# Chunk 0's graph attention moved into the last but one attention iteration, chunk 1's into the recurrence's first half

## The chip, the cores and the metric

One core of one Trainium2 chip runs the kernel. The metric is the device time of one execution in microseconds; the kernel before takes 1593.96 us (median of 3 runs, 1591.88 to 1594.06).

## The reference, cut to what matters

Input x is 128 graphs of 64 tokens with 256 features; adj is one 64x64 adjacency for all. Four residual blocks follow one another, each on `h = relu(layernorm(x))`:

```python
x = x + L0(h)   # attention, 8 heads, q/k/v/o products, scores masked by adj
x = x + L1(h)   # attention, 8 heads; o + layernorm(o) * gamma + beta
x = x + L2(h)   # graph attention: hw = h @ W
                # e = leaky_relu(s1[i] + s2[j], 0.2) * adj; att = softmax(e)
                # elu(att @ hw + beta * hw)
x = x + L3(h)   # gated recurrence, 3 steps:
                # av = [adj h, adj h];  z = sigmoid(av w3 + h u3)
                # r = sigmoid(av w4 + h u3);  hv = tanh(av w5 + (r*h) u5)
                # h = (1-z)*h + z*hv
```

## The kernel before, in words

x stays in on-chip memory as 64 tiles of 128 tokens; four tiles (8 graphs) are a chunk, so there are 16 chunks (`CHUNKS`). The engines run separate programs, one block each (`@block.tensor` and so on), and meet at semaphores. The order on each engine is written by hand; nothing is scheduled by a planner.

**Attention.** One software-pipelined loop (`iterations`, `body(i, ...)`) runs over T = 32 chunk-steps: 16 of L0, then 16 of L1. In iteration i the tensor engine (PE) makes the scores of i, transposes the softmax output p of i-1 (`p_transposes`), transposes the normalised rows of i+1, projects the output of i-2 (`o_products`), multiplies p by v for i-1 (`values`) and projects q, k, v of i+1. The vector engine (DVE) masks and takes maxima (`mask_and_max`), sums, makes the low parts of split operands (`o_low`), takes outputs (`take_first`, `take_out`), makes statistics (`o_stats`) and adds the normalised output (`final_sum`). The scalar engine (ACT) copies out of PSUM, takes exponentials and normalises. POOL subtracts maxima (`shift`), divides (`normalise`), turns statistics into rstd (`norms`, `norm`), scales by gamma (`scale`) and issues two accumulating DMAs (`beta_to_x`, `o_to_x`). Each fp32 product is three matmuls of high and low parts (`product`, line 99).

**PSUM** has two tensors of four banks: `scores`, also called `high`, and `ring`. A p transpose of the drained pipeline (i = T) writes ring banks 0 and 1 only when the oT held there has been read by `o_low`.

**Graph attention** of chunk c: `graph_rows` transposes normalised rows, `graph_high`/`graph_low` split them into g_hT, four `graph_product` make hw, `graph_s2` makes s2, `graph_scores` e and its maximum, `g_shift` and `g_exponential` the exponential, `graph_attention` att, `graph_attT` transposes it, `copy_attT` adds beta times identity, `graph_aggregate` makes y, and `graph_out` on ACT and DVE applies elu and adds to x. Chunks 2 to 15 are done inside the recurrence, but chunks 0 and 1 stand in the tail behind the attention loop.

**Recurrence.** Two chunks are in flight; a *half* is half a step's work for one of them (`half(s)`, `halves`). `enter` brings a chunk in from its normalised rows (r_hn). Half 0 starts chunk 0 with `hu = u3 hp`, the neighbour sums with adjT (`agg`), then w4 (r), w3 (z) and w5; the next half starts with hu of chunk 1 and then `u5` on r*h (rhp) of chunk 0. In the tail, the graph attention of chunks 0 and 1 and the last attention iterations T-1, T, T+1 are interleaved by a hand-written list per engine; on PE it begins:

```python
iterations(pe, body)
scores_piece(T - 1)
p_transposes(T - 1, 1)
o_products(T - 1, 1)
pe.wait_ge(s_masked, (T - 1) * R + 2)
graph_rows(0, high)
values(T - 1, 1)
```

## Time and profile before

| | us |
|---|---|
| median of 3 runs | 1593.96 |
| lowest, highest | 1591.88, 1594.06 |
| the profiled execution | 1595.16 |
| its span, first to last instruction | 1593.1 |
| PE busy | 1510.5 (95%) |
| DVE busy | 1243.9 (78%) |
| ACT busy | 993.0 (62%) |
| POOL busy | 533.7 (34%) |

The span is 2.06 us shorter than the profiled execution's own time, which is 1.2 us above the median. Attention fills the span up to about 600 us and the recurrence from about 640 us. Busy shares are of the span; a wait is idle time of an engine, put down to the instruction that released it. The granted clock of PE is given as a share of 2.4 GHz. All times below are from the start of the span.

### The profile page before, as it was taken

What the parts mean: (1) busy time and instruction counts of PE and PEld (TensorE: products, weight loads), DVE (VectorE), ACT (ScalarE), POOL (GpSimd) and SP (SyncE); (2) the same over time, 40 slices, a digit from 0 to 9 for tenths busy, and PEclk for the clock granted to TensorE, in tenths of its full rate; (3) what the DMA queues carried; (4) which work ended last, traced back from release to release, by engine and by line L of the source; (5) the groups of instructions that cost most, each with busy time, mean ns of one, the idle gap of its engine ahead of it and who ended that gap; (6) DMA issues with size and microseconds to landing.
All of it is one profiled execution on the core that took longest, in us unless ns stands there. A gap on an engine that the chain in (4) does not pass through costs nothing.

```text
span 1593.1 us, 40455 instructions
## 1 busy us (share of the span) xinstructions
PE 1510.5 (95%) x16248; PEld 1299.4 (82%) x16248; DVE 1243.9 (78%) x2511; ACT 993.0 (62%) x1793; POOL 533.7 (34%) x622
## 2 busy tenths in 40 slices
PE   3899999899999987799999999999999999999997
PEld 3789989798888876588888888888888888888885
DVE  2787887988899986677877877877777777778666
ACT  3676677667777774565666566655665566566553
POOL 1666766667787893300101111111111111111000
PEclk9999999999999998899999999999999999999998
DMA  9200000003322242100000000000000000000000
GB/s 251 82 3 0 0 0 1 15 16 61 61 53 53 56 78 29 27 0 1 27 1 1 27 0 0 26 0 0 26 0 0 26 0 0 27 1 0 27 1 26
DMA packets 36760, 40.12 MB, mean 25 GB/s; under 512 B 11840, under 2 KB 31808, under 8 KB 36672
## 3 DMA queue, kind: packets, MB, share of 16 engines
q0 software_dynamic: 4608, 16.78, 5.6%
q1 hardware_dynamic: 32064, 22.10, 4.8%
q8 instruction: 64, 1.05, 0.3%
q14 instruction: 24, 0.20, 0.0%
HBM read 13.71 MB, written 8.39 MB: 14 GB/s over the span
## 4 chain that ended last, share of the span: by engine, by line
PE 68%; DVE 15%; ACT 7%; issue 5%; POOL 4%; DMA 1%; SPq 0%; DVEq 0%; POOLq 0%; ACTq 0%
PE ring L99 30%; PE scores L99 23%; PE scores L1545 3%; PE ring L1343 2%; PE scores L1307 2%; DVE rhp_lo L1196 2%; PE ring L1490 2%; DVE total L955 2%; POOL s L530 1%; PE ring L1380 1%; ACT rhp_hi L824 1%; ACT later_w L814 1%; PE ring L1508 1%; PE ring L1463 1%; ACT later_w L808 1%
## 5 line engine op out<-in xcount | busy, mean ns | idle before, releaser
L1196 DVE TENSOR_TENSOR rhp_lo<-r,rhp_hi 128x1024 fp32r<-128x1024 f32 x48 | 58.8, 1225 | 157.0 <-ACT rhp_hi L824 157.0
L530 POOL TENSOR_TENSOR s<-s,mx 128x512 f32<-128x512 f32 x128 | 137.9, 1102 | 46.3 <-DVE mx L951 46.3
L536 POOL TENSOR_TENSOR s<-s,rtotal 128x512 f32<-128x512 f32 x128 | 131.4, 1056 | 36.7 <-DVE rtotal L957 36.5
L594 POOL TENSOR_TENSOR r_var_eps<-r_mean_var,eps 128x4 f32<-128x4 f32 x16 | 8.1, 509 | 384.3 <-DVE r_mean_var L1105 384.3
L669 ACT ACTIVATE s<-s 128x512 f32<-128x512 f32 x128 | 78.4, 644 | 76.1 <-POOL s L530 75.9
L839 ACT ACTIVATE hv<-scores,bias 128x512 f32<-128x512 f32 x96 | 66.1, 689 | 83.6 <-PE scores L99 83.6
L946 DVE SCALAR_TENSOR_TENSOR s<-scores,mask 128x512 f32<-128x512 f32 x128 | 87.2, 681 | 32.4 <-PE scores L1307 32.4
L808 ACT ACTIVATE later_w<-ring 128x512 f32<-128x512 f32 x64 | 34.8, 595 | 121.9 <-PE ring L1508 121.9
L681 ACT ACTIVATE pT<-ring 128x512 f32<-128x512 f32 x128 | 66.1, 604 | 47.1 <-PE ring L1343 47.1
L951 DVE TENSOR_REDUCE mx<-s 128x8 f32<-128x512 f32 x128 | 87.9, 686 | 4.4
L857 ACT ACTIVATE r<-r,bias_half 128x512 f32<-128x512 f32 x96 | 64.3, 717 | 37.7 <-DVE r L1221 37.7
L99 PE MATMUL scores<-rhp_hi,u5T_hi 128*128 128x512 f32 x192 | 80.4, 419 | 4.0 <-DVE rhp_lo L1196 1.8
L955 DVE TENSOR_REDUCE total<-s 128x8 f32<-128x512 f32 x128 | 82.6, 645 | 0.0
L1232 DVE TENSOR_TENSOR later_w<-scores,hu 128x512 f32<-128x512 f32 x96 | 64.4, 686 | 19.6 <-PE scores L99 18.8
L99 PE MATMUL ring<-agg_hi,w4T_hi 128*128 128x512 f32 x192 | 78.9, 411 | 0.0
L99 PE MATMUL scores<-agg_hi,w3T_hi 128*128 128x512 f32 x192 | 78.3, 408 | 0.0
L594 POOL TENSOR_TENSOR g_var_eps<-g_mean_var,eps 128x4 f32<-128x4 f32 x16 | 7.3, 457 | 209.5 <-DVE g_mean_var L1105 209.5
L99 PE MATMUL scores<-agg_hi,w5T_hi 128*128 128x512 f32 x192 | 77.0, 401 | 0.0
L99 PE MATMUL ring<-agg_lo,w4T_hi 128*128 128x512 f32 x192 | 76.2, 397 | 0.0
L99 PE MATMUL ring<-agg_hi,w4T_lo 128*128 128x512 f32 x192 | 76.2, 397 | 0.0
L99 PE MATMUL scores<-agg_hi,w5T_lo 128*128 128x512 f32 x192 | 75.9, 395 | 0.0
L99 PE MATMUL scores<-rhp_lo,u5T_hi 128*128 128x512 f32 x192 | 75.8, 395 | 0.0
(295 smaller groups left out, 5251.2 us busy)
## 6 DMA issues: line engine op xcount, KB each, us to landing
x<-beta_less_one POOLq DMA_DIRECT2D x16, 512.0 KB, 4.6
x<-o POOLq DMA_DIRECT2D x16, 512.0 KB, 6.5
out_x<-x SPq DMA_DIRECT2D x16, 512.0 KB, 2.9
x<-in_x SPq DMA_DIRECT2D x1, 6656.0 KB, 30.5
later_w<-in_L_gnn_w_w SPq DMA_DIRECT2D x3, 512.0 KB, 7.2
x<-in_x SPq DMA_DIRECT2D x1, 1024.0 KB, 10.9
stage<-in_L_gnn_w_qkv SPq DMA_DIRECT2D x3, 256.0 KB, 3.0
x<-in_x SPq DMA_DIRECT2D x1, 512.0 KB, 3.5
```

The source lines that it names most:

```text
L99: last = pe.matmul(out, s, m, start=(begins and n == 0), stop=(ends and n == len(terms) - 1))
L530: pool.tensor_tensor(sr, sr, mx[:, r, :].unsqueeze(2).to_broadcast([P, CT * 2, N]), ALU.subtract).then_inc(s_shifted, 1)
L536: pool.tensor_tensor(sr, sr, rtotal[:, r, :].unsqueeze(2).to_broadcast([P, CT * 2, N]), ALU.mult).then_inc(p_ready, 1)
L669: act.activation(s[:, par, r, :, :, :], s[:, par, r, :, :, :], ACT.Exp).then_inc(p_exp, 1)
L681: act.activation(pT[:, r, :, :].rearrange("p t q -> p (t q)"), ring[:, r, :], ACT.Copy).then_inc(pT_copied, 1)
L839: act.activation(hv[:, m, :], high[:, 2 + m, :], ACT.Tanh, bias=bias[:, 2, m:m + 1])\
L857: act.activation(r[:, m, :], r[:, m, :], ACT.Tanh, bias=bias_half[:, 1, m:m + 1], scale=0.5)\
L946: dve.scalar_tensor_tensor(sr(par, r), scores[:, r, :].rearrange("p (a k) -> p a k", k=N), SCALE, masks[layer_of(i, lay)][:].unsqueeze(1). ...
L951: dve.reduce_max(mx[:, r, :], sr(par, r), AX.X).then_inc(s_max, 1)
L955: dve.reduce_sum(total[:, r, :], sr(par, r), AX.X).then_inc(p_total, 1)
L1196: dve.tensor_tensor(rhp.lo[:], r[:], f32(rhp.hi[:]), ALU.subtract).then_inc(rh_lo_ready, 1)
L1232: dve.tensor_tensor(z[:, m, :], high[:, m, :], hu[:, m, :], ALU.add).then_inc(z_added, 1)
```

## The change

Chunk 0's graph attention starts in `body(T - 2)`: rows normalised first on ACT, transposed on PE behind the values, split into new buffers (`g_hT_first`, in the part of later_w that is free by then), multiplied between the k and v products. The rest of chunk 0 stands in iteration T-1; chunk 1's products in iteration T. Chunk 1's attT transpose, aggregate, output and entry are moved into the recurrence's first half. On ACT the last two `o_normalise` move into that half; on DVE the last three `final_sum` stand behind the first half (one) and the second (two). `hw_next` and `h_a` get other places in memory; `enter`, `graph_high`, `graph_low` and others take the PSUM bank as an argument.

```diff
@@ placement
+        g_hT_first = Parts(plan, "g_hT_first", [P, FT, CW], start["later_w"] + 4096)
-        hw_next = sb("hw_next", [P, CT, WX], F32, start["s"] + 8192)
+        hw_next = sb("hw_next", [P, CT, WX], F32, start["w_ext"])
-        h = [sb(f"h_{q}", [P, FT, CW], F32, start["o_n"] + 4096 * n) for n, q in enumerate("ab")]
+        h = [sb("h_a", [P, FT, CW], F32, start["w1o_hi"]), sb("h_b", [P, FT, CW], F32, start["o_n"])]
@@ ACT, body
+                    if isinstance(i, int) and i == T - 2:
+                        graph_normalise(0, 0)
                     o_normalise(i, par, lay)
...
+                        if i == T - 2:
+                            graph_high(0, high, 0, g_hT_first)
...
+                        if isinstance(i, int) and i == T - 2:
+                            for t in range(CT):
+                                copy_hw(0, t, high, 2)
                         copy_v(i + 1, 1 - par)
@@ ACT, half
+                    if s.first:
+                        o_normalise(T + 1, 1, 1)
...
+                    if s.first:
+                        graph_out(1, high, 2)
+                        norm_rows(rn, r_hn[1], 1, 1)
+                        enter(1, 1)
                     if s.graph_norm is not None:
                         graph_normalise(s.graph_norm, 0 if s.k == 0 else 1)
+                    if s.first:
+                        o_normalise(T + 2, 0, 1)
@@ DVE, body
+                    if isinstance(i, int) and i == T - 2:
+                        graph_low(0, high, 0, g_hT_first)
                     o_stats(i, par, lay)
                     final_sum(i, par, lay)
+                    if isinstance(i, int) and i == T - 2:
+                        rows_stats(gn, 1, x_final)
@@ DVE, half
+                    if s.first:
+                        copy_attT(1, high, 2)
...
+                    if s.first:
+                        graph_out(1, high, 2)
+                        recurrence_stats(1)
...
+                    if s.first:
+                        enter(1, 1)
@@ DVE, behind the halves
                     half(s)
                     if s.first:
+                        final_sum(T + 1, 1, 1)
+                    if isinstance(s.n, int) and s.n == 1:
                         final_sum(T + 2, 0, 1)
                         final_sum(T + 3, 1, 1)
                         dve.wait_ge(x_final, CHUNKS)
@@ PE, body
+                    if i == T - 2:
+                        pe.wait_ge(s_masked, (i + 1) * R)
+                        graph_rows(0, high)
...
+                        if isinstance(i, int) and i == T - 2:
+                            pe.wait_ge(g_hT_lo_ready, FT)
+                            pe.wait_ge(gw_lo_ready, 2)
+                            for t in range(CT):
+                                wait(pe, hw_copied, t - 1)
+                                graph_product(0, t, high, 2, g_hT_first)
@@ PE, half
+                    if s.first:
+                        graph_attT(1, high, 2)
...
+                    if s.first:
+                        graph_aggregate(1, high, 2, hw_next)
...
+                        if s.first:
+                            pe.wait_ge(x_plus_pos, 4)
                         for m in range(FT):
                             product(pe, high[:, 2 + m, :], columns(wT["w5"], m), moving(agg), ends=False)
+                    if s.first:
+                        pe.wait_ge(hu_copied, FT)
+                        enter(1, 1)
@@ PE, tail
                 scores_piece(T - 1)
                 p_transposes(T - 1, 1)
+                pe.wait_ge(s_masked, (T - 1) * R + 1)
+                graph_s2(0, high, 0, g_hT_first)
                 o_products(T - 1, 1)
...
                 values(T - 1, 1)
...
+                graph_attT(0, high, 0)
                 pe.wait_ge(s_masked, T * R)
...
+                graph_rows(1, high, 2)
+                graph_aggregate(0, high, 0)
                 p_transposes(T, 0)
...
                 pe.wait_ge(g_hT_lo_ready, 2 * FT)
                 for t in range(CT):
                     if t >= 2:
                         pe.wait_ge(hw_copied, CT + t - 1)
...
+                    graph_product(1, t, high, 2)
+                o_products(T, 1)
+                graph_s2(1, high, 2)
+                values(T, 0)
                 o_products(T + 1, 1)
...
                 pe.wait_ge(x_plus_pos, 2)
...
+                enter(0, 0, high, 0)
                 halves(pe, half)
@@ POOL, tail
+                norms(T - 1, 1, 1)
+                norm(gn, 1, 1)
                 pool.wait_ge(v_ready, T * 2)
+                pool.memset(att[:], 0.0).then_inc(att_cleared, 1)
                 pool.memset(adjT[:], 0.0).then_inc(adj_cleared, 1)
...
+                shift(T - 1, 1, 0)
+                shift(T - 1, 1, 1)
+                g_shift(0)
+                beta_to_x(T - 1, 1)
+                o_to_x(T - 1, 1, 1)
+                shift(T - 1, 1, 2)
+                shift(T - 1, 1, 3)
+                scale(T - 1, 1, 1)
+                for q in range(R):
+                    normalise(T - 1, 1, q)
+                norm(rn, 0, 0)
```

The order on DVE in iteration T-1, before, from its last mask to the second split of graph rows (L951 maximum, L973 o_low, L1114 graph_low):

```order
L951 TENSOR_REDUCE mx<-s 128x8
L966 TENSOR_TENSOR o<-ring,out_bias_93 128x512
L973 TENSOR_TENSOR oT_lo<-ring,oT_hi 128x4x2x64 x2
L955 TENSOR_REDUCE total<-s 128x8
L957 RECIPROCAL rtotal<-total 128x8
L955 TENSOR_REDUCE total<-s 128x8
L957 RECIPROCAL rtotal<-total 128x8
L1114 TENSOR_TENSOR g_hT_lo<-scores,g_hT_hi 128x512 x2
```

o_low stands right behind the last output and ahead of the sums. After the change, the same place from the last mask on (L972 maximum, L1175 copy_attT, L976/L978 a sum, L1183/L1188 graph_out, L1125 statistics, L994 o_low):

```order
L972 TENSOR_REDUCE mx<-s 128x8
L1175 TENSOR_TENSOR attT<-scores,beta_ident 128x512
L987 TENSOR_TENSOR o<-ring,out_bias_93 128x512
...
L1183 SCALAR_TENSOR_TENSOR x<-scores,x 128x512 x2
L1188 TENSOR_TENSOR x<-x,later_w 128x1024
...
L1125 BN_STATS r_stats<-x 128x6 x4
L1128 MEMSET carrier 128x1
L1130 BN_AGGR r_mean_var<-r_stats 128x2 x4
L987 TENSOR_TENSOR o<-ring,out_bias_93 128x512
L994 TENSOR_TENSOR oT_lo<-ring,oT_hi 128x4x2x64 x2
```

Two sums stand in each of the first two gaps. o_low now comes behind the four sums, chunk 0's graph output and its statistics.

The order on ACT around the first half, before (L692 o_normalise, L768 normalised rows, L818/L829 the hu copies, L835 agg_hi):

```order
L801 ACTIVATE h_a<-scores 128x512
L692 ACTIVATE o_n<-o,shift_by,rstd 128x256 x4
L768 ACTIVATE r_hn_b<-x,r_shift_by,r_rstd 128x256 x4
L692 ACTIVATE o_n<-o,shift_by,rstd 128x256 x4
L818 ACTIVATE hu<-ring 128x512
L829 ACTIVATE hu<-ring 128x512
L835 ACTIVATE agg_hi<-scores 128x512 x2
```

and after the change (L706 o_normalise, L789 normalised rows, L839/L850 the hu copies, L856 agg_hi, L813/L816 chunk 1's graph_out):

```order
L822 ACTIVATE h_a<-scores 128x512
L706 ACTIVATE o_n<-o,shift_by,rstd 128x256 x4
L839 ACTIVATE hu<-ring 128x512
L850 ACTIVATE hu<-ring 128x512
L856 ACTIVATE agg_hi<-scores 128x512 x2
L706 ACTIVATE o_n<-o,shift_by,rstd 128x256 x4
L880 ACTIVATE r<-r,bias_half 128x512 x2
L813 ACTIVATE later_w<-scores 128x512 x2
L816 ACTIVATE later_w<-later_w 128x1024
L789 ACTIVATE r_hn_b<-x,r_shift_by,r_rstd 128x256 x4
```

One block of four stands ahead of the hu copies instead of three; chunk 1's rows are normalised behind r.

## Rows read from the trace of the kernel before

**Rows 1.** Stretches: us, busy PE PEld DVE ACT POOL, PEclk, DMA share, GB/s.

```profile
583.60:672.00 88.40, 62.01 (x706) 54.66 (x706) 59.67 (x141) 49.18 (x95) 39.34 (x54) 0.85 0.25 37
...
672.00:1560.00 888.00, 882.71 (x4642) 739.89 (x4642) 687.73 (x1215) 535.47 (x929) 87.52 (x122) 1.00 0.03 9
```

**Rows 2.** PE's waits in 583 to 672 us: total, times, longest.

```profile
PE ring L1463 <- ACT hu L829: 9.2, 1, 9.2
...
PE scores L1482 <- DVE att L1143: 6.6, 2, 4.8
...
PE scores L99 <- DVE g_hT_lo L1114: 5.9, 1, 5.9
```

**Rows 3.** Stretches again, same columns, for the granted clock (PEclk).

```profile
599.03:604.80 5.77, 5.77 (x26) 5.67 (x27) 4.45 (x15) 1.37 (x4) 4.95 (x8) 0.50 0.18 1
...
614.84:624.30 9.46, 9.46 (x66) 8.85 (x66) 6.12 (x11) 4.11 (x8) 0.61 (x1) 1.00 0.00 0
...
629.20:642.10 12.90, 8.89 (x26) 6.85 (x27) 8.36 (x20) 5.48 (x10) 0.79 (x3) 0.63 0.00 1
...
654.83:659.50 4.67, 4.67 (x15) 3.78 (x16) 2.97 (x11) 2.97 (x6) 2.39 (x4) 0.50 0.21 39
```

**Rows 4.** The same view: the graph products, and the twelve w3 matmuls.

```profile
615.25:618.25 3.00, 3.00 (x28) 3.00 (x26) 1.46 (x3) 1.16 (x3) 0.00 (x0) 1.00 0.00 0
...
660.88:663.68 2.80, 2.80 (x14) 2.26 (x13) 2.48 (x4) 2.18 (x5) 0.00 (x0) 1.00 0.00 0
```

**Rows 5.** PE's timeline: start us, us, line, operation, count, [idle before].

```profile
583.60 1.59 PE L1307 MATMUL scores<-kT,qT 32*64 32x64 f32 x128
...
585.12 1.97 PE L1343 MATMUL ring<-ident,s 128*128 128x128 f32 x16
...
639.38 0.80 PE L99 MATMUL ring<-hp_a_hi,u3T_hi 128*128 128x512 f32 x1 [3.16 <-DVE hp_a_lo L1168]
...
671.86 0.48 PE L99 MATMUL scores<-rhp_hi,u5T_hi 128*128 128x512 f32 x1
```

**Rows 6.** DVE's timeline, same columns.

```profile
582.76 1.62 DVE L1000 TENSOR_TENSOR x<-x,o_n 128x1024 f32<-128x1024 f32 x1
...
597.73 1.24 DVE L1114 TENSOR_TENSOR g_hT_lo<-scores,g_hT_hi 128x512 fp32r<-128x512 f32 x2
...
606.22 0.86 DVE L1123 TENSOR_TENSOR e<-scores,hw 64x256 f32<-64x256 f32 x2 [2.54 <-PE scores L99]
...
608.03 0.42 DVE L1132 TENSOR_REDUCE g_mx<-e 128x4 f32<-128x256 f32 x1
...
612.93 1.85 DVE L1143 TENSOR_TENSOR att<-e,g_rtotal 64x256 f32<-64x256 f32 x2
...
624.71 1.41 DVE L1100 BATCH_NORM_STATS2 r_stats<-x 128x6 f32<-128x256 f32 x4
...
628.28 0.85 DVE L1143 TENSOR_TENSOR att<-e,g_rtotal 64x256 f32<-64x256 f32 x2
...
664.49 2.35 DVE L1000 TENSOR_TENSOR x<-x,o_n 128x1024 f32<-128x1024 f32 x2
...
691.76 1.22 DVE L1196 TENSOR_TENSOR rhp_lo<-r,rhp_hi 128x1024 fp32r<-128x1024 f32 x1 [3.63 <-ACT rhp_hi L824]
```

**Rows 7.** ACT's timeline, same columns.

```profile
575.42 0.63 ACT L669 ACTIVATE s<-s 128x512 f32<-128x512 f32 x1 [0.98 <-POOL s L530]
...
635.60 1.06 ACT L795 ACTIVATE later_w<-later_w 128x1024 f32<-128x1024 f32 x1
...
643.00 2.08 ACT L692 ACTIVATE o_n<-o,shift_by,rstd 128x256 f32<-128x256 f32 x4 [4.40 <-POOL shift_by L524]
```

**Rows 8.** POOL's timeline, same columns.

```profile
611.72 2.36 POOL L560 TENSOR_TENSOR o_n<-o_n,gamma 128x1024 f32<-128x1024 f32 x1 [2.57 <-ACT o_n L692]
...
647.94 0.19 POOL L594 TENSOR_TENSOR r_var_eps<-r_mean_var,eps 128x4 f32<-128x4 f32 x1
...
649.48 0.20 POOL L600 TENSOR_TENSOR r_shift_by<-r_minus_mean,r_rstd 128x4 f32<-128x4 f32 x1
```

More of the change, by code:

```diff
@@ L567, in body @@
                         norm(gn, 0, 0)
-                    if isinstance(i, int) and i == T - 1:
-                        norm(gn, 1, 1)
                     if exists(i):
@@ L843, in half @@
                         copy_hw(s.graph_a, 1)
-                    if s.enters is not None:
+                    if s.enters is not None and not s.first:
                         enter(s.enters, s.other)
+                    if s.first:
+                        o_normalise(T + 1, 1, 1)
                     if s.norm is not None and s.k == 4:
@@ L1249, in _ @@
                 iterations(dve, body)
-                rows_stats(gn, 1, x_final)
-                for q in range(3):
-                    mask_and_max(T - 1, 1, q, 1)
-                take_first(T - 1, 1, 1)
-                mask_and_max(T - 1, 1, 3, 1)
+                mask_and_max(T - 1, 1, 0, 1)
+                mask_and_max(T - 1, 1, 1, 1)
+                graph_scores(0, high, 0)
+                mask_and_max(T - 1, 1, 2, 1)
+                dve.wait_ge(att_cleared, 1)
+                dve.tensor_scalar(beta_ident[:], ident[:], g_beta[:, 0:1], None, ALU.mult).then_inc(beta_ident_ready, 1)
@@ L1255, in _ @@
+                graph_attention(0)
+                mask_and_max(T - 1, 1, 3, 1)
+                dve.wait_ge(beta_ident_ready, 1)
+                copy_attT(0, high, 0)
+                take_first(T - 1, 1, 1)
+                sums(T - 1, 1, 0)
+                sums(T - 1, 1, 1)
+                graph_out(0, high, 0)
+                sums(T - 1, 1, 2)
+                sums(T - 1, 1, 3)
+                recurrence_stats(0)
                 take_out(T - 3, 1, 1, 1)
                 o_low(T - 2)
-                sums(T - 1, 1, 0)
@@ L1258, in _ @@
-                sums(T - 1, 1, 1)
-                graph_low(0, high)
-                sums(T - 1, 1, 2)
-                sums(T - 1, 1, 3)
+                graph_low(1, high, 2)
                 o_stats(T - 1, 1, 1)
-                final_sum(T - 1, 1, 1)
-                dve.tensor_scalar(beta_ident[:], ident[:], g_beta[:, 0:1], None, ALU.mult).then_inc(beta_ident_ready, 1)
-                graph_scores(0, high, 2)
-                graph_low(1, high)
                 take_first(T, 0, 1)
                 take_out(T - 2, 1, 0, 1)
-                dve.wait_ge(att_cleared, 1)
@@ L1270, in _ @@
-                graph_attention(0)
+                o_stats(T, 0, 1)
+                final_sum(T - 1, 1, 1)
+                graph_scores(1, high, 2, hw_next)
                 o_low(T - 1)
-                dve.wait_ge(beta_ident_ready, 1)
-                copy_attT(0, high, 2)
-                graph_scores(1, high, 0, hw_next)
-                graph_out(0, high, 2)
-                recurrence_stats(0)
+                graph_attention(1)
                 take_first(T + 1, 1, 1)
                 take_out(T - 1, 1, 1, 1)
-                graph_attention(1)
@@ L1280, in _ @@
-                copy_attT(1, high, 0)
+                enter(0, 0, high, 0)
+                o_stats(T + 1, 1, 1)
                 final_sum(T, 0, 1)
-                graph_out(1, high, 0)
-                enter(0, 0, high)
-                o_stats(T, 0, 1)
-                recurrence_stats(1)
-                o_stats(T + 1, 1, 1)
-                final_sum(T + 1, 1, 1)
-                dve.wait_ge(x_final, CHUNKS - 2)
-                halves(dve, first_half)
+                dve.wait_ge(x_final, CHUNKS - 4)
@@ L1291, in _ @@
+                halves(dve, half_and_rest)
             @block.tensor
@@ L1539, in half @@
                         if s.first:
-                            pe.wait_ge(x_plus_pos, 4)
                             pe.wait_ge(adj_loaded, 32)
@@ L1554, in half @@
                         pe.wait_ge(hu_copied, (n + 1) * FT)
-                    if s.enters is not None:
+                    if s.enters is not None and not s.first:
                         enter(s.enters, s.other)
+                    if s.first:
+                        graph_attT(1, high, 2)
                     if s.graph_a is not None:
```

112 lines of the change are left out of this document (45 added, 67 removed).

## The prediction

> **What bounds the kernel now.** Read the busy time by stretch first [rows 1]: from 672 us on the tensor engine (PE) works 882.71 of 888.00 us, so whatever is won or lost before is carried to the end unchanged; in 583.6 to 672 us, where the change sits, it works only 62.01 of 88.40. The list of waits and the timeline say where the other 26 us go [rows 2, 5]: four releasers make up 24.9 us, the longest single wait being 9.2 us for the scalar engine's (ACT) copy of hu. The granted clock adds a second loss [rows 3]: after the waits of 5.9 and 9.2 us matmuls ran at the lower of the two levels (0.50, 1.2 GHz), for 5.77 us after the first and 4.67 us after the last, while after the 1.8 us wait for the first att the clock stayed at 1.00. Between 629.2 and 642.1 us, behind the 4.8 us wait for the second att, it was 0.63 in the mean, with work broken by waits of 0.9 and 3.2 us.
>
> **Unit prices.** The 24 graph products of 128x258 took 3.0 us and twelve matmuls of 128x512 2.80 us (0.233 each) [rows 4]; from the first of these I take 2.85 for the 24 projection matmuls of 128x256 and 1.45 for 16 of half the size. 16 transposes cost up to 1.9 us, the scores 1.5 [rows 5]. At the lower clock each doubles. Vector engine (DVE): one PSUM subtraction or bias add of 128x512 0.6, the graph score block 2.25, statistics of one chunk 1.75, a 128x1024 addition 1.25; a mask and its maximum 1.3, a sum and its reciprocal 0.8, from the same widths [rows 6]. ACT: four rows of 128x256 2.0, a 128x1024 pass 1.0, a 128x512 one half of it [rows 7]. The norm steps on POOL take 1.74, from 647.94 to 649.68 [rows 8].
>
> **The sum, station by station**, on the clock of the profiled execution. T is 32.
>
> 1. *Iteration T-2.* PE gets 8 transposes (0.95) after the values, and 24 graph products (2.9) between k and v. ACT normalises the graph rows (2.0) ahead of o_normalise and the exponentials; the wait for POOL's shift that stood there (0.98 [rows 7]) covers half of it, so o_high and the last exponential are 0.9 later. DVE runs its four sums and then graph_low (1.2 for both halves), which ends at 583.05; PE reaches the products at 581.75 and so waits 1.3. Scores of T-1 start at 583.60+0.95+1.3+2.9 = 588.75, **5.15 later** than now.
> 2. *Iteration T-1.* Scores 1.5, transposes 1.9, graph_s2 1.4: 593.55. On DVE graph scores 2.25, mask 2 1.3, beta_ident 0.25, attention 1.5 (two att instructions of 0.43, a sum, a reciprocal), mask 3 1.3, copy_attT 0.65: 600.85. PE meanwhile runs its projections and values and waits 1.1 for att. Aggregate 1.6: 602.5. The two waits for the graph's own chain (5.9 and 1.8) have become one of 1.1, and the half-clock products of now run at full clock in T-2.
> 3. *The new hole.* The transposes of T need o_low(T-2), which on DVE stands behind first output 0.6, two sums 1.6, graph_out(0), two sums 1.6, recurrence statistics 1.75, an output 0.6. graph_out ends at 606.3 (ACT, which has two exponentials and graph_high(1) before them, ends its relus and Exp at 605.05; then the addition). So the first half of o_low ends at 610.85 and PE idles **8.35**. That is longer than any wait now before the first half, and the lower clock follows as it did after 5.9.
> 4. PE from 610.85: 16 transposes at half clock 3.45, products of chunk 1 eleven slow and thirteen fast 3.95, projection 2.85, s2 1.4, values 1.45: 623.95. DVE then does output, statistics of o 1.85, final_sum 1.25, graph_scores(1) 2.25 and o_low(T-1) 1.2, ending 628.3; PE idles 4.35 and, as after 4.8 now, comes back slow: projection of T+1 5.1, entry transposes 1.5, four ACT copies and DVE's hp_a_lo: 636.85. Now the recurrence's first product starts at 639.38 [rows 5], so up to here only **2.5** is won.
> 5. *First half.* Now ACT keeps PE 9.2 waiting, because o_normalise, norm_rows and o_normalise stand ahead of the hu copies [rows 2, 7]. After the change one o_normalise (2.0) stands there and fits under the products. hu 2.8, neighbour sum 1.85, agg_hi and agg_lo 1.15, w4 2.8, aggregate(1) 1.6, w3 2.8, w5 2.8: PE ends at 652.6, now 666.5. But chunk 1 isn't in yet: from its y at 647.0 relus and Exp 2.25, addition 1.25, statistics 1.75, POOL 1.75, norm_rows 2.05, transposes, ACT copies and hp_b_lo 3.25: 659.3. PE idles 3.5 and 2.2 around the transposes; I take the clock low behind this.
> 6. *Second half.* hu twelve slow 5.1, graph transposes and neighbour sum 2.7: 667.1. On ACT graph rows 2.0, o_normalise 2.0, z 1.3, hu 0.5, rhp_hi 1.0 after 658.65, then DVE's rhp_lo 1.25: 666.7. The u5 product, which starts at 671.86 now [rows 5], starts at **667.0**: 4.9 won.
> 7. *Sharing between DVE and POOL.* The addition x<-x,o_n took 1.2 alone (two in 2.35) and 1.62 beside POOL work; the pair of att took 0.85 alone and 1.85 beside POOL's 2.36 us scaling [rows 6, 8]. In stations 2 to 4 POOL's shifts, scale and normalise stand beside the att and addition. Between nothing and 1.4 us, I take 0.7, since the first att meets DMA issues rather than scaling.
>
> All moved pieces exist in both: 8+8 transposes, 48 products, the Exps, the additions, the POOL DMAs (two in each of T-1 and T, one in T+1 and T+2), the SP queue's adjT loads. The memset that starts the latter comes some 10 us earlier and the product that needs them only at 640. New buffers (hw_next, h_a, g_hT_first) add no instruction. I cost at nothing: final_sum(T+1), 1.2, now behind the first half on DVE, and the last two final_sums (2.35 together, now after the first half, then after the second [rows 6]); what hides them there is DVE's wait of 3.63 before rhp_lo. If that cover is gone, they cost up to 2.35.
>
> Sum: 4.9 - 0.7 = **4.2 us** less. The profiled execution took 1595.16 (span 1593.1, 2.06 around it), the median is 1593.96; against the median that is **1589.8**, 0.26% faster. The bound for "same" is 0.2%, 3.2 us: about what a measurement of this kernel can tell from no change.
>
> **Rivals.**
> *A, the gain is mostly given back in the second half.* DVE enters it late, with one 1.2 us final_sum before and 2.35 behind; the 3.63 us cover is partly used up by ACT being 0.7 us later than now against PE's u5. Then 2.35 more shows: 4.2 - 2.35 = 1.85 won, 1592.1. For it: the wait for rhp_hi is the last thing before u5. Against: after 672 us DVE is busy 77% only [rows 1].
> *B, the 4.35 us wait of station 4 leaves the clock high.* It is shorter than the 4.8 that the clock fell with; the 1.8 us wait left it at 1.00 [rows 2, 3]. Projection and transposes of station 4 then cost 3.6 and not 6.6, minus what ACT has to do anyway: 2.3 more won, 1587.5.
> *C, slower: the clock stays low through the first half.* It did so now over 12.9 us, with work cut up by short waits [rows 3]; the changed first half has waits of 1.95 and 0.65. If the clock doesn't return before w4, hu costs 2.8 more, the neighbour sum 1.8 and w4 2.8, 0.7 of it hidden: 6.7 lost against 4.2 won, 1596.5. It decides at 637 us: the clock must be back by the first hu. Against: 6.6 us of unbroken work stand ahead of that, and in both unbroken stretches of now the clock came back, after 5.77 and 4.67 us [rows 3].
> *D, POOL and DVE block each other whole:* the pair of att then waits for all of a POOL instruction like the 2.36 us scaling, and the two additions lose 0.43 each [rows 6, 8]: 3.2 instead of 0.7, so 1.7 won, 1592.3. Against: the slowest att pair on record lost 1.0. SBUF — State Buffer in the Trainium skill (section Who interferes with whom) has this rule: a DVE instruction with two SBUF inputs and a GpSimd instruction that reads SBUF lock each other out for the whole instruction. The trace agrees that the two meet, with 1.85 against 0.85, and not yet with the full length.
>
> **Numbers.** Forecast 0.47, A 0.18, B 0.15, C 0.10, D 0.10. The range from 1586.0 to 1595.0 takes in the forecast, A, B and D with a microsecond or more of room, and leaves out C. Faster by over 0.2%: forecast 0.43, B 0.14, a part of A and D 0.03: 0.60. Same: 0.32. Slower: 0.08.
>
> **What would show it.** In the changed profile: a wait of PE for g_hT_lo near 582 us of 1 to 2 us; scores of T-1 near 588.8; the longest wait (7 to 10 us) on the transposes of T, released by DVE's oT_lo; the first u3 product near 637; hardly a wait for hu; 3 to 4 us for r_hn_b's transposes behind the first w5; u5 near 667; PE 1.00 busy from there. It is wrong if the hole is over 11 us, if the first u3 product is not before 639.4, or if waits in the loop grow.

## The result, and the profile after

| | before | changed |
|---|---|---|
| median | 1593.95 us (4 runs, 1591.88 to 1594.06) | 1603.88 us (4 runs, 1600.81 to 1607.28) |
| ratio | | 1.0066 [1.0044, 1.0088] |
| profiled execution | 1595.16, span 1593.1 | 1607.28, span 1605.2 |

The change is **slower**, by 0.66%; 1603.88 lies outside the range given. The profiled execution of the changed kernel is the slowest of its four, so its profile shows 12.1 us of difference where the medians show 9.9.

First the stretches of the changed kernel, beside [rows 1]: iteration T-2 from its scores to those of T-1, from there to the first u5 product, and 888 us behind it (us, busy time of PE, PEld, DVE, ACT and POOL, PEclk, DMA share, GB/s).

```profile
572.71:595.47 22.76, 21.22 (x385) 19.26 (x384) 20.00 (x53) 15.88 (x32) 19.72 (x26) 1.00 0.25 48
595.47:683.46 87.99, 60.47 (x673) 52.85 (x673) 53.02 (x125) 44.72 (x84) 35.73 (x48) 0.79 0.25 37
683.46:1571.46 888.00, 882.36 (x4635) 739.47 (x4636) 691.40 (x1218) 535.98 (x930) 87.81 (x122) 1.00 0.03 9
```

The recurrence is as before: PE works 882.36 of 888 us, against 882.71. The stretch from the scores of T-1 to u5 takes 87.99 us where it took 88.26 (583.60 to 671.86 [rows 5]), so the 5.36 us that T-2 has grown by aren't earned back. I call the whole from the scores of T-2 to the first u5 product **the tail**: 105.66 us before (from 566.20 to 671.86), 110.75 after. PE's waits in it (engine, line, released by: total, times, longest):

```profile
PE ring L1375 <- DVE oT_lo L994: 7.6, 1, 7.6
PE ring L99 <- DVE hp_a_lo L1193: 6.2, 1, 6.2
PE ring L99 <- DVE oT_lo L994: 4.6, 1, 4.6
PE ring L1504 <- ACT r_hn_b L789: 3.6, 1, 3.6
PE scores L1523 <- DVE att L1168: 2.3, 1, 2.3
PE ring L99 <- DVE hp_b_lo L1193: 2.0, 1, 2.0
PE scores L99 <- DVE g_hT_first_lo L1139: 1.4, 1, 1.4
PE ring L99 <- DVE agg_lo L1229: 1.0, 1, 1.0
```

Of the waits of before [rows 2], the one for hu is gone, those for att are down to one of 2.3 and the one for g_hT_lo to 1.4. The hole on o_low(T-2) is there as foreseen. The second line is not in the sum at that size. It stands between these two rows of PE's timeline, the first product of T+1 and the first u3:

```profile
637.16 0.55 PE L99 MATMUL ring<-w1o_hi,oT_hi 128*128 128x256 f32 x1 [4.60 <-DVE oT_lo L994]
...
649.41 0.80 PE L99 MATMUL ring<-hp_a_hi,u3T_hi 128*128 128x512 f32 x1 [6.23 <-DVE hp_a_lo L1193]
```

The timelines of DVE and ACT show what it is:

```profile
635.72 1.29 DVE L994 TENSOR_TENSOR oT_lo<-ring,oT_hi 128x512 fp32r<-128x512 f32 x2
...
646.87 1.29 DVE L987 TENSOR_TENSOR o<-ring,out_bias 128x512 f32<-128x512 f32 x2 [8.44 <-ACT o_n L706]
648.08 1.28 DVE L1193 TENSOR_TENSOR hp_a_lo<-scores,hp_a_hi 128x512 fp32r<-128x512 f32 x2
```

```profile
643.75 0.60 ACT L821 ACTIVATE hp_a_hi<-scores 128x512 fp32r<-128x512 f32 x1
644.23 0.62 ACT L822 ACTIVATE h_a<-scores 128x512 f32<-128x512 f32 x1
644.71 2.08 ACT L706 ACTIVATE o_n<-o,shift_by,rstd 128x256 f32<-128x256 f32 x4
```

`take_first(T + 1)` on DVE writes the buffer `o` that `o_normalise(T)` on ACT reads. The change puts that o_normalise behind `enter(0, 0, high, 0)` on ACT, and take_first stays ahead of enter on DVE. (The text on the change ahead of the prediction says that the last two o_normalise move. A third moves too, this one: in the kernel before it stands ahead of `g_exponential(0)` and is done at 611.6, 28 us before the first u3.) So ACT must finish the entry of chunk 0 and then 2.08 us of rows before DVE may begin two subtractions that PE is waiting for. Its input had been ready since POOL's shift at 625.1.

A second part of the difference stands where no code was changed. From the first scores of the program to those of T-2 the profile of before takes 532.07 us and this one 539.20. PE's granted clock there, in two stretches of the changed kernel and then in the same two of the kernel before:

```profile
300.00:320.00 20.00, 17.02 (x324) 15.24 (x327) 16.67 (x41) 10.82 (x21) 13.56 (x17) 0.83 0.09 28
420.00:440.00 20.00, 19.30 (x306) 17.11 (x306) 14.46 (x38) 12.50 (x25) 12.62 (x14) 0.83 0.14 26
```

```profile
300.00:320.00 20.00, 16.77 (x351) 15.12 (x349) 18.37 (x45) 11.66 (x23) 12.70 (x16) 1.00 0.10 29
420.00:440.00 20.00, 20.00 (x366) 17.89 (x365) 18.75 (x47) 16.01 (x32) 15.93 (x17) 1.00 0.28 53
```

So of the 12.1 us between the two profiled executions 5.1 are the tail, 7.1 lie ahead of the change, and the ends cancel. What the second part is had to be asked as well.

### The profile page after: what moved, and what is told of

The parts are those of the page before. It is cut to its first block, busy times and chain, and to the rows that moved or that the text cites. A ratio compares the mean times of both kernels' runs of the same rounds, so it can differ in the third digit from the quotient of the medians.

```text
span 1605.2 us, 40456 instructions
## 1 busy us (share of the span) xinstructions
PE 1519.1 (95%) x16248; PEld 1306.1 (81%) x16248; DVE 1244.1 (78%) x2511; ACT 994.3 (62%) x1793; POOL 534.5 (33%) x622
## 4 chain that ended last, share of the span: by engine, by line
PE 70%; DVE 13%; ACT 8%; issue 4%; POOL 3%; DMA 1%; SPq 0%; DVEq 0%; POOLq 0%; ACTq 0%
PE ring L99 32%; PE scores L99 23%; PE scores L1585 3%; PE ring L1375 3%; PE scores L1336 2%; DVE rhp_lo L1221 2%; PE ring L1412 2%; ACT rhp_hi L845 2%; PE ring L1531 2%; ACT later_w L835 1%; DVE total L976 1%; ACT later_w L829 1%; PE ring L1504 1%; PE ring L1549 1%; POOL s L531 1%
## 5 line engine op out<-in xcount | busy, mean ns | idle before, releaser
L829 ACT ACTIVATE later_w<-ring 128x512 f32<-128x512 f32 x64 | 34.8, 596 | 121.0 <-PE ring L1549 121.0
L972 DVE TENSOR_REDUCE mx<-s 128x8 f32<-128x512 f32 x128 | 87.9, 686 | 4.4
L976 DVE TENSOR_REDUCE total<-s 128x8 f32<-128x512 f32 x128 | 82.5, 645 | 0.0
L99 PE MATMUL scores<-rhp_hi,u5T_lo 128*128 128x512 f32 x192 | 75.8, 395 | 0.0
L99 PE MATMUL scores<-agg_hi,w3T_lo 128*128 128x512 f32 x192 | 75.8, 395 | 0.0
```

The source lines that it names most:

```text
L99: last = pe.matmul(out, s, m, start=(begins and n == 0), stop=(ends and n == len(terms) - 1))
L972: dve.reduce_max(mx[:, r, :], sr(par, r), AX.X).then_inc(s_max, 1)
L976: dve.reduce_sum(total[:, r, :], sr(par, r), AX.X).then_inc(p_total, 1)
```

## Experiments

In all profiles the way from the first u5 to the end takes 921.2 to 922.6 us, so the tail can be read by itself. Beside every run below stand 17 to 29 executions of the kernel before, from which its ratio is taken; their medians were 1593.4 to 1594.6. "Up to scores T-2" counts from the first scores of the program.

| kernel | median us (runs) | ratio [95%] | up to scores T-2 | tail |
|---|---|---|---|---|
| before, again | 1594.08 (10) | 0.9990 [0.9975, 1.0005] | 531.7 | 105.6 |
| change, again | 1602.02 (10) | 1.0050 [1.0028, 1.0071] | 534.1 | 110.0 |
| e1 o_n first | 1594.04 (10) | 0.9990 [0.9973, 1.0007] | 531.8 | 107.1 |
| e6 o_low alone | 1593.97 (10) | 1.0007 [0.9998, 1.0016] | 532.0 | 103.2 |
| e2 both orders | 1587.83 (4) | 0.9957 [0.9941, 0.9974] | 532.8 | 97.7 |
| e3 first half only | 1594.17 (10) | 0.9997 [0.9985, 1.0009] | 537.2 | 101.2 |
| e4 e2 + o_low(T-1) | 1586.56 (12) | 0.9955 [0.9939, 0.9970] | 533.3 | 95.3 |
| e5 e2 + added work | 1583.30 (6) | 0.9937 [0.9923, 0.9952] | 532.3 | 94.2 |
| e9 change + added work | 1594.67 (10) | 1.0006 [0.9993, 1.0019] | 531.9 | 104.2 |
| e8 e4 + e5 | 1581.07 (6) | 0.9918 [0.9902, 0.9934] | 530.9 | 92.9 |
| e7 change, 305 us | 1597.03 (11) | 1.0015 [1.0004, 1.0027] | 530.8 | 110.6 |
| e10 before, 305 us | 1591.17 (12) | 0.9979 [0.9966, 0.9991] | 528.5 | 106.1 |

### Both kernels again

> The kernel before as a kernel of its own, for a second trace. Theory U: the scores of T-2 may come late here too in one run or another (568 us or more). Theory L: 566.2 within 0.5 us. The ratio to the kernel before is 1.000 within 0.002.

> The changed kernel once more, untouched. Theory U (part of the loss lies ahead of the change and comes and goes): the scores of iteration T-2, at 572.7 us in the first profile against 566.2 before, start elsewhere this time, and the time moves with them by as much. Theory L (the loss ahead of the change belongs to this program): again 572 to 573 us and 1601 to 1607. Both: from the scores of T-2 to the first u5 product again about 110.7 us, against 105.7 before.

The tails repeat within 0.8 us: 105.6 and 110.0. The part ahead doesn't: 531.7 and 534.1, after 532.1 and 539.2. The ten runs of the changed kernel spread from 1596.5 to 1609.1, and they go with the granted clock: its mean over an execution is 0.987 to 0.989 in the three fastest (up to 1597.2) and 0.979 in the two slowest (1608.8 and 1609.1). The kernel before has 1590.8 to 1598.8 in its ten, but 1590.6 to 1603.2 in the 25 beside them, so the spread alone doesn't tell the two kernels apart.

### e1: o_normalise(T) ahead of the entry

```diff
 ACT:
                 o_high(T - 1)
+                o_normalise(T, 0, 1)
                 g_exponential(1)
                 enter(0, 0, high, 0)
-                o_normalise(T, 0, 1)
```

> The changed kernel with o_normalise(T) ahead of g_exponential(1) and enter(0) on ACT instead of behind them. Theory W (DVE's output of T+1 waits for this normalisation, which stands behind chunk 0's entry): the 8.4 us wait of DVE for o_n goes, PE's wait for hp_a_lo falls from 6.2 to 1 to 2.5 us, the first u3 product comes 4 to 6 us earlier against the scores of T-2, and the time falls by 4 to 9 us against the changed kernel (up to 3 more than the wait, since hu then may run at the full clock). Rival (the order on ACT is harmless, PE at half clock sets the pace from 637 us on): less than 1.5 us.

One moved line: tail 107.1, 3.0 to 3.7 us less than the change, and the time is that of the kernel before. The timelines of PE, DVE and ACT:

```profile
631.07 0.55 PE L99 MATMUL ring<-w1o_hi,oT_hi 128*128 128x256 f32 x1 [4.59 <-DVE oT_lo L994]
...
639.70 0.79 PE L99 MATMUL ring<-hp_a_hi,u3T_hi 128*128 128x512 f32 x1 [2.44 <-DVE hp_a_lo L1193]
```

```profile
636.42 0.69 DVE L987 TENSOR_TENSOR o<-ring,out_bias 128x512 f32<-128x512 f32 x1 [1.62 <-PE ring L99]
```

```profile
627.56 2.07 ACT L706 ACTIVATE o_n<-o,shift_by,rstd 128x256 f32<-128x256 f32 x4
```

o_n is done at 629.6, take_first waits for PE and no longer for ACT, and PE's wait for hp_a_lo falls from 6.2 to 2.4. From the product of T+1 to the first u3 it is 8.63 us where the change takes 12.25. That the misplaced o_normalise costs 3 to 4 us of the tail is shown. The first u3, counted from the scores of T-2, comes 2.2 to 2.9 us earlier and not the 4 to 6 expected, since the way up to the product of T+1 was 0.7 to 1.3 us longer in this profile (its aggregate products took 3.49 us against 2.70, being slow for longer). The time fell by 8.0; the other 4 to 5 us aren't in the tail.

### e2 and e6: o_low(T-2) ahead of chunk 0's output

```diff
 DVE:
                 take_first(T - 1, 1, 1)
+                take_out(T - 3, 1, 1, 1)
                 sums(T - 1, 1, 0)
                 sums(T - 1, 1, 1)
-                graph_out(0, high, 0)
                 sums(T - 1, 1, 2)
                 sums(T - 1, 1, 3)
-                recurrence_stats(0)
-                take_out(T - 3, 1, 1, 1)
                 o_low(T - 2)
                 graph_low(1, high, 2)
+                graph_out(0, high, 0)
+                recurrence_stats(0)
```

e2 has this on top of e1, e6 has it alone.

> e1 with o_low(T-2) and graph_low(1) on DVE ahead of chunk 0's graph output and its statistics. Theory H (the 7.6 us wait of PE for o_low is made by this order): the wait falls to 3 to 4.5 us and 4 to 6 us are won on e1, if nothing else steps in. Rival (chunk 0's entry chain, output, statistics, norm rows, becomes the last one): PE's wait moves to r_hn_a or hp_a_lo and less than 2 us are won.

> The change with e2's edit of DVE's order alone (take_out(T-3) and o_low(T-2) ahead of chunk 0's graph output, sums and graph_low(1)); ACT keeps o_normalise(T) behind chunk 0's entry. If the two losses stand one behind the other in one chain, they add: e1's edit is worth 8.0 us of time (3 to 3.7 of it on the way from the scores of T-2 to the first u5), e2's 9.4 on that way, so this one has 110.4 - 9.4 = 101 us on it and a time of 1590.5 to 1592.5. If the wait for o_normalise(T) takes back what the earlier o_low(T-2) gives (DVE stands at take_first(T+1) until the same moment), 104 to 106 us and 1594 to 1597.

PE's waits for oT_lo, of e2 and then of e6:

```profile
PE ring L1375 <- DVE oT_lo L994: 2.2, 1, 2.2
```

```profile
PE ring L99 <- DVE hp_a_lo L1193: 6.2, 1, 6.2
...
PE ring L1375 <- DVE oT_lo L994: 1.7, 1, 1.7
```

The hole falls from 7.6 to 2.2 and 1.7. e2's tail is 97.7, 9.4 less than e1's and more than was expected, and its time is 0.4% under that of the kernel before: chunk 0's output and statistics can wait some 4 us, since only the entry needs them, while PE stands at o_low. e6 has a tail of 103.2 and was expected at 101. The 6.2 us wait for hp_a_lo stays there, as it must with o_normalise(T) where it was, so the loss of o_low's place and that of o_normalise's place stand one behind the other. Alone the edits are worth 3.0 to 3.7 and 6.9 to 7.6, together 12.4 to 13.1, about 2 us over the sum. About 1 us of that lies behind the first u3: from there to u5 it is 33.3 us in e1 and e6 and 32.3 in e2, where the first u3 products are no longer at half clock. e6's time, 1593.97, is over what was expected, and over what its tail says: by that alone it should be 2.5 us under the kernel before. Its profiled execution, one of the two fastest of ten, took 1592.4; why the median is higher is open.

### e3: the first half's part alone

This kernel begins chunk 0's attention where the kernel before does and has its order of T-1, but ends chunk 1's in the first half, with both o_normalise there.

> The first half's part of the change alone, on the order of before: chunk 1's attention ends inside the recurrence's first half, o_normalise of T+1 and T+2 stand there too, h_a lies in its new place; nothing of chunk 0's attention begins in iteration T-2, and ACT has o_normalise(T) ahead of g_exponential(0) as before. From the scores of T-2 to the first u5 the kernel before takes 105.7 us and the change 110.0 to 110.8. Theory W (the loss is one late instruction of ACT, o_normalise(T) behind the entry of chunk 0, which this kernel doesn't have): the att wait of 6.6 goes, 2 to 3 of it come back as waits for the entry and in the first half, so 102 to 105 us and a time of 1590 to 1593.5. Rival F (the first half is what costs: chunk 1's end there makes PE wait and run at half clock for more than the 6.6 us that are saved): 106 us or more, 1594 to 1598, with the first u3 early and the way from it to u5 35 us or longer (32.5 before, 34.05 in the change).

PE's waits:

```profile
PE scores L1487 <- ACT r_hn_a L782: 6.2, 1, 6.2
PE scores L99 <- DVE g_hT_lo L1132: 6.0, 1, 6.0
PE ring L1487 <- ACT r_hn_b L782: 3.6, 1, 3.6
```

Tail 101.2, 4.5 less than before: this part of the change is a gain by itself, from the scores of T-1 to the first u3 50.3 us against 55.8, and Rival F's "u5 35 us behind the first u3" didn't come (33.6). So the loss of the change is in how it orders T-2 to T+1, not in the first half. Yet the median is that of the kernel before, and over the 1590 to 1593.5 expected. In the profile the part ahead took 537.2. The ten runs lie at 1589.97 to 1593.17 (five) and 1595.17 to 1596.87 (five), the profile being of the upper ones, so that the part ahead hides the gain in half of the runs is likely and not shown: there is no profile of a lower one.

### e4: o_low(T-1) ahead of graph_scores(1)

```diff
 DVE:
                 final_sum(T - 1, 1, 1)
+                o_low(T - 1)
                 graph_scores(1, high, 2, hw_next)
-                o_low(T - 1)
```

> e2 with one more step of DVE's order: o_low(T-1) ahead of graph_scores(1). It looks for the next wait of the chain, the 4.6 us of PE in front of o_products(T+1). If DVE's order makes that wait, it falls to about 2.4 (graph_scores(1) is 2 us of DVE work) and the time is 1584.5 to 1587 (e2: 1587.8). If instead graph_attention(1), which is that much later, becomes the next to be waited for in the first half (its attT stands behind hu), PE waits there 1 to 2 us more and the time stays at 1587 to 1589.

PE's wait in front of o_products(T+1) went from 4.6 to 2.3, and the tail by 2.3 us to 95.3. Nothing waits for the later attention of chunk 1. Time 1586.56, within what was expected, though the gain over e2 is smaller than the spread of either.

### e5 and e9: added work in the waits

```diff
 PE, tail and first half:
                 values(T, 0)
+                pe.wait_ge(x_done, (T - 1) * 2)
+                filler(2, 38)
                 o_products(T + 1, 1)
                 pe.wait_ge(x_plus_pos, 2)
                 enter(0, 0, high, 0)
+                filler(0, 18)
...
                         pe.wait_ge(hu_copied, FT)
+                        filler(2, 28)
                         enter(1, 1)
+                        pe.wait_ge(r_added, FT)
+                        filler(0, 16)
```

`filler(bank, n)` is n transposes of the identity into a free bank of `ring`; nobody reads them. e5 adds them to e2, e9 to the changed kernel (50 in place of 18).

> e2 with transposes of the identity on PE, whose results nobody reads: 38 in front of o_products(T+1), 18 behind the transposes of chunk 0's entry, 28 in front of chunk 1's entry in the first half and 16 behind it, where PE waits in e2 for 4.6, 2.0, 3.6 and 2.0 us. It measures what the half clock costs that comes with these waits (rival C of the prediction, a half clock through the first half). If the half clock is a cost of its own: granted clock 1.00 in the first half (about .70 to .80 in e1 and e2), 3 to 5 us less from the wait to u5, 1583 to 1585. If the waits alone count, since what is waited for isn't PE's work: no change, 1587 to 1589; where the added transposes outlast the waits, up to 2 us longer, 1589 to 1590.

> The changed kernel with e5's added transposes in the waits of its last stretch (38, 50, 28 and 16; the second is longer than in e5, since the wait for hp_a_lo is 6.2 us here) and nothing else. It prices the half clock in the change itself, apart from its waits. From the scores of T-2 to the first u5 the change takes 110.0 to 110.8 us. If the price is e5's (3.5 us there) and a little more for the first u3, which runs at half clock behind the 6.2 us: 105.5 to 107 us, time 1597 to 1600. If only the waits count: 110 us, 1602 to 1604.

From the scores of T-1 to the first u3, and from there to u5: first e9, then the change without it, then e5 and e2.

```profile
588.68:639.30 50.62, 38.50 (x641) 35.77 (x640) 35.22 (x82) 24.54 (x48) 24.55 (x33) 0.93 0.37 54
639.30:670.17 30.87, 27.27 (x164) 23.37 (x165) 18.09 (x44) 19.97 (x36) 11.21 (x15) 1.00 0.09 18
```

```profile
595.47:649.41 53.94, 33.10 (x554) 30.55 (x553) 34.95 (x82) 24.77 (x48) 24.54 (x33) 0.77 0.35 51
649.41:683.46 34.05, 27.36 (x120) 22.30 (x121) 18.07 (x44) 19.95 (x36) 11.19 (x15) 0.81 0.08 16
```

```profile
588.48:628.98 40.50, 35.22 (x610) 32.11 (x609) 34.95 (x82) 24.90 (x48) 24.46 (x33) 0.96 0.46 66
628.98:659.84 30.86, 27.26 (x164) 23.36 (x165) 18.07 (x44) 19.96 (x36) 11.19 (x15) 1.00 0.11 21
```

```profile
588.80:631.30 42.50, 30.58 (x554) 28.03 (x553) 34.95 (x82) 24.77 (x48) 24.43 (x33) 0.88 0.44 64
631.30:663.63 32.33, 25.77 (x120) 21.16 (x121) 19.04 (x45) 20.67 (x37) 11.19 (x15) 0.84 0.09 17
```

With 100 to 132 more instructions on PE the work ends earlier. In the changed kernel the half clock costs 3.3 us up to u3 and 3.2 from there to u5, 6.5 in all (5.8 against the second profile of the change). In e2, whose first u3 comes behind a 2.4 us wait and not behind 6.2, it costs 2.0 and 1.5. The added work produces nothing that anyone reads, and PEclk is 1.00 from the first u3 to u5 in both, so the kept clock is what wins.

The Trainium skill's page "TensorE: Matmul & The Clock Gate" (Terms) prices the loss as the throttled time times one minus the granted share, in other words as if all of that time were work. For e2's 32.33 us at a mean clock of 0.84 (some 10.3 us of it at 0.50) that is an estimate of 5.2 us. The measurement, 1.5, decides. PE has work in 25.77 of these 32.33 us, so a part of the slow time was waiting; that another part ran beside ACT and DVE chains that ended later anyway is likely, and no run splits the two.

e9's tail, 104.2, and its time, 1594.67, are both under what was expected, and with it the changed kernel is back at the kernel before. e5's 1583.30 is as expected.

### e8: e4 and e5 together

18, 18, 28 and 16 transposes, since the first wait is shorter.

> e4 and e5 together (o_low(T-1) ahead of graph_scores(1), and 18, 18, 28 and 16 added transposes, fewer ahead of o_products(T+1), since the wait there is 2.3 us). Scores of T-2 to first u5: e4 95.3, e5 94.2. If the shorter wait and the kept clock add: 91.5 to 93 us and 1580.5 to 1582.5. If they are the same microseconds (what e4 won was mostly covered by e5's clock): 93.5 to 94.5 and 1582.5 to 1584.

Tail 92.9 and time 1581.07, so the two gains mostly add. This is the best version run: **0.8% under the kernel before** (ratio 0.9918 [0.9902, 0.9934]), 1.3% to 1.4% under the changed one's two medians.

### e7 and e10: the part ahead of the change

```diff
 PE, o_products:
                         pe.wait_ge(oT_lo_ready, (c + 1) * 2)
+                        if g == 1 and isinstance(i, int) and i == CHUNKS - 1:
+                            for _ in range(20):
+                                pe.transpose(ring[:, 3, 0:P], ident[:], ident[:])
                         rows_product(oT, ...)
```

PE waits there for hT_lo, behind weight work on DVE, in the kernel before too. In the changed kernel:

```profile
304.81 0.58 PE L99 MATMUL ring<-w0o_hi,oT_hi 128*128 128x256 f32 x1 [2.98 <-DVE hT_lo L1076]
```

e7 is the changed kernel with these 20 transposes, e10 the kernel before with them.

> The changed kernel with 20 transposes of the identity (results unread) on PE ahead of the second half of the output product of iteration CHUNKS-1, where PE waits 3.0 us for hT_lo at about 302 us in every profile, before and after alike. In the profiles of the change, and of e3, the granted clock is 0.83 in 300 to 320 us and the next scores come 2.0 us later than in the profiles of the kernel before, where it stays 1.00. Theory U (half-clock spells in unchanged code ahead of the change, at this wait and at two waits of PE for nothing shown at about 400 and 420 us, make the spread of runs and 3 to 4 us of the change's median over what its last stretch explains): clock 1.00 in 300 to 320, the scores of iteration CHUNKS 21.3 us behind those before them, the median 1 to 2 us under the change's 1602 to 1604, 1600 to 1602.5, and the lowest runs as before (1596 to 1597). If this spell isn't what costs: 1602 to 1604 unchanged.

> The kernel before with e7's 20 transposes in the same place, so that the two kernels are compared with the unchanged part ahead of the change alike. In e7 the change ran in 1596.1 to 1598.0 us, median 1597.0, where it has 1600.8 to 1607.3 and 1596.5 to 1609.1 without them. If the change's own last stretch is worth the 4.4 to 5.1 us that the profiles give it, and the rest of its median were half-clock spells ahead: this one runs within 3 us too, with a median of 1591.5 to 1593, so e7 is 4 to 5.5 us over it. If the kernel before gains as much as the change did (5 us or more), 1589 or less, and the change costs 8 us wherever the rest is.

In e7 the stretch that had a clock of 0.83:

```profile
300.00:320.00 20.00, 19.84 (x381) 18.38 (x380) 18.35 (x46) 12.72 (x26) 12.94 (x16) 1.00 0.09 29
```

Its runs lie at 1596.1 to 1598.0, where they lay at 1596.5 to 1609.1 without; the median fell by 5.0 to 6.9 us, more than expected, with the tail unchanged (110.6). The lowest run is the same. e10 gained 2.3 (1591.17, a little under what was expected, from 1593.42 of the kernel before beside it), and its runs lie within 3.9 us where the 17 beside them lie within 8.1.

But the added transposes did more than keep the clock. They also ended two waits 90 to 110 us later, at the first passes of the second attention loop, which both kernels have and the profile gives no releaser for. Here is that group in the change; neither e7 nor e10 has such a wait between 380 and 445 us.

```profile
L1412 PE MATMUL ring<-pT,v 64*32 64x64 f32 x384 | 5.0, 228 | 4.9 <-issue 4.9
```

The way from one iteration's scores to the next shows where the time goes. The columns are the iterations whose scores come at 297, 318, 407 and 426 us in the kernel before; the transposes are added in the one that ends at 318, and the waits without a releaser are in the last two:

| kernel | to 297 | to 318 | to 407 | to 426 |
|---|---|---|---|---|
| before | 20.38 | 21.33 | 19.05 | 19.15 |
| before, again | 20.46 | 21.24 | 19.31 | 18.80 |
| e10 before, 305 us | 20.47 | 21.24 | 17.40 | 17.52 |
| change | 20.40 | 23.39 | 20.90 | 22.80 |
| change, again | 21.36 | 21.27 | 19.33 | 20.64 |
| e7 change, 305 us | 21.49 | 20.20 | 17.33 | 17.54 |

In e10 nothing is won where the transposes are (the clock was 1.00 there in the kernel before too); nearly all of its gain, 3.3 of 3.6 us, is in the last two columns, where the two waits, 3.7 us in the kernel before, are gone. In the change those columns hold 4.9 us of waits in the first profile and 3.9 in the second, which are gone in e7, and slow work besides. So the table shows that the first profile of the change loses 7.6 us to the kernel before in three iterations of unchanged code, with the clock at 0.83 to 0.93 there and 1.2 us more of waits, and that this comes and goes: the second profile loses 2.7 in the four. It doesn't show how much of e7's 5.0 to 6.9 us is the kept clock and how much the two waits, and no run adds 20 instructions where PE has no wait, which would tell them apart.

With the transposes in both, the two kernels stand **5.9 us** apart (1597.03 and 1591.17, with 1593.90 and 1593.42 for the kernel before beside them). The tails of their profiles give 4.5 of that. The last 1.4 are open: 2.3 more ahead of T-2 and 1.0 more behind u5 in e7's profile (of its execution of 1598.0 us) than in e10's (1590.6). The 2.3 are not at the places of the table; 2.2 of them are in the first and the fourth iteration of the loop.

Why the changed kernel's median has 3.5 to 4.8 us from ahead of T-2, by the same instructions up to there, no run shows.

## Why the prediction was wrong

It said 4.2 us won in the tail, 1589.8. Measured are 4.4 to 5.1 lost there, and in the medians another 3.5 to 4.8 that the tail doesn't hold. One of its own signs of being wrong came: the first u3 product is not before 639.4 but at 649.41, and counted from the scores of T-2 it is 76.7 us where it was 73.2.

**Station 1** was right: PE waited 1.41 for graph_low (1.3 foreseen), the scores of T-1 came 5.36 later (5.15).

**Stations 2 and 3** were right in kind. The hole is 7.59 (8.35), with PE at half clock behind it. But it ends 24.2 us after the scores of T-1 and not 22.1. PE's timeline, with the idle time before each:

```profile
606.94 0.66 PE L1523 MATMUL scores<-ident,att 128*128 128x128 f32 x4 [2.35 <-DVE att L1168]
...
609.42 2.70 PE L1531 MATMUL scores<-hw,attT 128*128 128x256 f32 x8
619.71 3.67 PE L1375 MATMUL ring<-ident,s 128*128 128x128 f32 x16 [7.59 <-DVE oT_lo L994]
```

The wait for att is 2.35 and not 1.1, and behind it the eight aggregate products already run slow (they end 2.70 us after their start; priced at 1.6). I had taken from [rows 2, 3] that a wait of this size leaves the clock high, as it did after 1.8 us. The att pair itself was mis-sized. It ran beside POOL (DVE's timeline, then POOL's):

```profile
604.83 2.05 DVE L1168 TENSOR_TENSOR att<-e,g_rtotal 64x256 f32<-64x256 f32 x2
```

```profile
604.48 1.68 POOL L531 TENSOR_TENSOR s<-s,mx 128x512 f32<-128x512 f32 x1
```

The pair costs 0.85 alone [rows 6], and this POOL subtraction 1.04. Station 7 took 0.7 for all such meetings; this one alone cost 1.2, a little more than the POOL instruction takes alone. Of the pair the first instruction took 1.62 and the second its usual 0.42, and the first ended 0.28 us behind the POOL one (606.44 and 606.16). The Trainium skill's page "SBUF — State Buffer" (Who interferes with whom) calls the port pair that the two engines share an exclusive lock. This row agrees with it: DVE's instruction ends as if it had begun when POOL's was done. That POOL's took 1.68 is mostly not the meeting: behind its two DMA issues the same subtraction takes 1.44 in the kernel before too (at 573.95), without att beside it. The other meetings that I had feared cost nothing (the second att pair took 0.85, the addition of chunk 0's output 1.22), so it is 1.2 in all, between my 0.7 and the 3.2 of rival D.

**Station 4 is where the sum broke.** Up to the wait for o_low(T-1) it held: 4.60 measured, 4.35 foreseen. From there to the first u3 I counted "projection of T+1 5.1, entry transposes 1.5, four ACT copies and DVE's hp_a_lo", 8.55 us; it took 12.25. The 3.7 us are take_first(T+1), which I had left out because its own work is small and PE feeds it early. It isn't its work that counts but its wait, for an instruction of ACT that the change moves to the end of ACT's list. I had followed what PE waits for, but not, for each DVE step ahead of hp_a_lo, what it waits for. e1 shows it: with the ACT instruction moved forward the same way takes 8.63 us, the 8.55 of the sum. Rival B did not come: behind the 4.60 us wait the 24 products of T+1 took 4.98, near the 5.1 of half clock.

**Stations 5 and 6** said 30.15 us from u3 to u5 and it took 34.05. The waits were right: no wait for hu (9.2 before), 3.6 and 2.0 around chunk 1's entry (3.5 and 2.2). The clock was wrong: "6.6 us of unbroken work stand ahead of that" was my reason against rival C. But station 4's miss put a 6.2 us wait in that place, and then the first half began slow. From the first u3 to the first w4 the sum has 5.8 us (hu 2.8, neighbour sum 1.85, agg 1.15), the change took 8.99 (to 658.40), and e9, at full clock, 6.24. So 2.75 of the 3.9 us are the half clock ahead of w4. (Over the whole way e9 is 3.2 shorter, but the slow hu of chunk 1 had been in the sum.) **Rival C** thus named the mechanism, with a price (6.7) of twice what was measured and a chance that was too low, 0.10. It went by the clock at the first hu, and there the u3 products did stand 0.43 us apart, but those of w4 stood 0.23 apart again. Of rival A nothing showed: DVE's wait for rhp_hi was still 3.72 us, behind the final_sum.

Together: 0.2 in T-2, 2.1 up to the end of the hole, 3.7 to u3, 3.9 to u5, less the 0.7 for sharing that stood in the sum, 9.2 us over the forecast of the tail.

**Outside the sum** were the 2 to 7 us ahead of the change (2.4 and 7.1 in the two pairs of profiles). The prediction held unchanged code for unchanged time. One profile of the kernel before, with the clock at 1.00 there, couldn't show that this differs from execution to execution.

## What to carry to other kernels

When an instruction is moved back on one engine, look for whoever overwrites what it reads or reads what it writes: the new wait often stands on another engine, at a small step ahead of the one that matters. Of two steps that are ready on a queue, the one that the tensor engine waits for goes first, even when the other started its chain earlier (9.4 us here for two moved steps). And a wait of TensorE can cost more than its length: in this kernel filling idle stretches of 2 to 6 us with work that nobody needs won 3.5 us of the tail in e2 and 5.8 to 6.5 in the change, where the work behind them was TensorE's own.

## What the runs showed of the hardware

- With 20 useless transposes in a wait of 3.0 us the runs of a 1.6 ms kernel spread over 1.9 us and not 12.6, and the median was 5 us lower. In part that is two waits some 100 us later that vanished with them, not the clock.
- The length of a wait alone doesn't say whether the clock falls. Behind a wait of 2.6 to 2.8 us that ends near 285 us in all fourteen profiles, the mean clock of 280 to 290 us was 1.00 in eight and 0.66 to 0.83 in six. At the next such place, from 300 to 320 us, it stayed at 1.00 behind 2.9 to 3.0 us in five profiles (both of the kernel before, e1, e5, e6) and was 0.83 behind 3.0 us in two (the change, e3); behind 1.9 and 2.0 us (e2, the change again) it was 0.91. These last two are of the six that were slow at 280 us already, which brought PE later to the second wait and made it shorter.
- Waits of PE without a releaser, 1.3 to 2.8 us each, stand at the first passes of a loop. The first is 1.8 to 2.1 us in every profile that has it, at either clock; the second was 2.55 and 2.80 in the two profiles with the lowest clock around it (e3, the change) and 1.3 to 1.9 in the others. Both vanished in the two kernels with added work some 100 us earlier, and the second also in e2, which has none there.
- The first of the att pair on DVE, beside POOL's subtraction (both read on-chip memory), took 1.62 us and not 0.42, and ended 0.28 us behind the POOL one. It took 1.61 to 1.62 us in all ten profiles that have this order.
